# Graph attention on one core: a tile's mask, queries and residual input are loaded from ScalarE's DMA queue in place of SyncE's

## The reference

```python
def _L0_gnn_ref(node_matrix, adjacency_matrix, Wks, Wqs, Wvs, Wo):
    adj = jnp.maximum(adjacency_matrix, jnp.eye(n))
    keys, queries, values = (jnp.einsum('nj,hjk->hnk', node_matrix, W) for W in (Wks, Wqs, Wvs))
    atts = jnp.einsum('hqk,hmk->hqm', queries, keys) / key_dim ** 0.5
    atts = atts - 1e+16 * (1.0 - adj)[None, :, :]
    atts = jax.nn.softmax(atts, axis=-1)
    return jnp.einsum('hqm,hmk,hko->qo', atts, values, Wo)

x = _layernorm(x + _L0_gnn_ref(x, adj, ...), axis=-1)     # layer 0
...                                                        # layers 1 to 3 follow on x
```

## Time and profile before

| | |
|---|---|
| median of 3 runs | 2812.24 us (2811.44 to 2812.98) |
| the profiled execution | 2815.72 us, its span 2813.9 us |
| PE, DVE, ACT, POOL busy over the span | 90%, 55%, 49%, 41% |
| attention stage | some 208 to 1495 us of the span |
| DMA queue of the kernel, share of 16 engines | 69.6% of the span |

### The profile page before, as it was taken

One profiled execution on the slowest core, in us unless ns is written; L12 is line 12 of the kernel. 1 busy time (PEld: TensorE's weight loads), 2 busy tenths in 40 slices (PEclk: granted clock), 3 DMA queues, 4 the chain that ended last, 5 costly groups with the idle time before them and its releaser, 6 DMA issues. The chain is left out here.

```text
span 2813.9 us, 67215 instructions
## 1 busy us (share of the span) xinstructions
PE 2536.2 (90%) x24716; PEld 1564.6 (56%) x24716; DVE 1534.5 (55%) x2860; ACT 1388.6 (49%) x1848; POOL 1163.6 (41%) x879
## 2 busy tenths in 40 slices
PE   7998898988889888898996999799999999979998
PEld 6875566656666566565663444376444444434443
DVE  3447677766777677676772222354454555633222
ACT  3337677767777677676772322223333334323221
POOL 0007687767777677776780032200111111110232
PEclk9999899988999999998998999899999999989999
DMA  3118999999999999999994356411656667742554
GB/s 124 63 57 171 179 174 174 166 174 171 160 173 166 180 173 166 166 181 169 174 157 130 117 196 206 167 48 42 161 153 168 174 178 205 187 127 80 199 196 151
DMA packets 870507, 436.18 MB, mean 155 GB/s; under 512 B 791680, under 2 KB 810112, under 8 KB 859008
## 3 DMA queue, kind: packets, MB, share of 16 engines
q1 hardware_dynamic: 870272, 432.93, 69.6%
HBM read 201.15 MB, written 38.44 MB: 85 GB/s over the span
## 5 line engine op out<-in xcount | busy, mean ns | idle before, releaser
L603 POOL TENSOR_TENSOR att_part_low<-att_scores,att_part_high 128x1024 f16<-128x1024 f32 x352 | 665.7, 1894 | 291.1 <-ACT att_part_high L735 265.2
L766 DVE CUSTOM_DVE_ANT_0 att_scores<-att_slots,att_adj 128x1024 f32<-128x1024 f32 x528 | 568.3, 1092 | 185.8 <-PE att_slots L641 167.1
L719 ACT ACTIVATE att_scores<-att_scores,att_nmax 128x1024 f32<-128x1024 f32 x528 | 531.2, 1037 | 65.8 <-DVE att_nmax L776 63.2
L641 PE MATMUL att_slots<-l_kk,att_q 128*128 128x512 f16 x2112 | 499.8, 376 | 46.4 <-issue 29.0
L1300 PE MATMUL a_ps<-l_y,a_adj 128*128 128x512 f16 (+1 forms) x1936 | 431.6, 382 | 9.0 <-DVE a_adj L1314 4.7
L661 PE MATMUL att_ps_pv<-l_vv,att_far_high 128*128 128x65 f16 x4928 | 270.8, 197 | 115.2 <-DMA att_far_low<-att_part_low 114.8
L661 PEld LDWEIGHTS att_ps_pv<-l_vv,att_far_high 128*128 128x128 f16 x4928 | 258.2, 101 | 159.3 <-DMA att_far_low<-att_part_low 128.6
L1300 PEld LDWEIGHTS a_ps<-l_y,a_adj 128*128 128x128 f16 (+1 forms) x1936 | 183.1, 98 | 257.5 <-issue 42.4
L641 PEld LDWEIGHTS att_slots<-l_kk,att_q 128*128 128x128 f16 x2112 | 190.9, 102 | 223.2 <-issue 77.2
L809 DVE TENSOR_TENSOR att_near_low<-att_ps_t,att_near_high 128x512 f16<-128x512 f32 x352 | 225.7, 681 | 133.5 <-ACT att_near_high L746 133.2
L1045 PE MATMUL edge_ps_o<-l_sup,edge_pt_high 128*128 128x512 f16 x968 | 288.1, 379 | 0.0
(11 more groups left out here) (149 smaller groups left out, 3842.6 us busy)
## 6 DMA issues: line engine op xcount, KB each, us to landing
l_adj<-in_adj_cols SPq DMA_DIRECT2D x44, 1408.0 KB, 6.2
att_adj<-in_adj SPq DMA_DIRECT2D x22, 1354.0 KB, 6.8
l_adj_tiles<-in_adj SPq DMA_DIRECT2D x22, 1354.0 KB, 6.0
p_x_in<-x SPq DMA_DIRECT2D x66, 256.0 KB, 2.6
att_q<-q_rows SPq DMA_DIRECT2D x88, 128.0 KB, 6.1
a_xres<-x SPq DMA_DIRECT2D x44, 256.0 KB, 2.7
scores_rows<-edge_raw SPq DMA_DIRECT2D x8, 842.0 KB, 3.5
p_x_in<-in_x SPq DMA_DIRECT2D x22, 256.0 KB, 2.7
```

Of the source, the lines that this page charges most:

```text
L603: nc.gpsimd.tensor_tensor(out=part[1][:, v, lo:lo + width], in0=sc[:, v, lo:lo + width], in1=part[0][:, v, lo:lo + width], op=ALU.subtract ...
L641: mm = nc.tensor.matmul(slots[:, slot, z:z + w], q[:, u, h % 2, a, h // 2, :], kk[:, h, lo + z:lo + z + w], start=a == 0, stop=a == 1)
L719: nc.scalar.activation(sc[:, v, lo:lo + width], sc[:, v, lo:lo + width], ACT.Exp, bias=nmax[:, v:v + 1]).then_inc(exp_done, 1)
L766: nc.vector.tensor_tensor_reduce(out=sc[:, v, lo:lo + width], in0=slots[:, (NC * h + c) % 2, 0:width], in1=adj[:, u, lo:lo + width], scale ...
```

## The change

The mask, the queries and the residual input are issued by ScalarE, at the end of its step h = 1, behind that step's copies of the near part. SP keeps the loads of the first tile, the transposes, and the store at the start of step h = 1. The waits that guard the loads go along with them.

```diff
+        def load_q(queue, t, u):
+            for e in range(2):
+                for half in range(2):
+                    queue.dma_start(q[half * KD:half * KD + KD, u, e, :, :, :].rearrange("p a j r -> p (a j r)"),
+                                    q_rows[bass.ds(t * P + e * KD, KD), :]).then_inc(q_loaded[u], 16)
+
         @block.sync
         def _(sp):
...
-            def loads(m, u):
-                t = 2 * m + u
-                if not is_tile(m, u, T) and not is_tile(m, u, T - 1):
-                    m1, u1 = after(m, u)
-                    if not is_tile(m, u, 0):
-                        sp.wait_ge(slot_free, PER_TILE * t)
-                    sp.dma_start(adj[:, u1, 0:N], adj_rows[bass.ds((t + 1) * P, P), :]) \
-                        .then_inc(adj_loaded[u1], 16)
-                    load_q(t + 1, u1)
-                if not is_tile(m, u, 0):
-                    if not is_tile(m, u, 1):
-                        sp.wait_ge(misc_free, 2 * (t - 1))
-                    sp.dma_start(xres[:, :], x_rows[bass.ds((t - 1) * P, P), :]).then_inc(xres_loaded, 16)
-                    if not is_tile(m, u, 1):
-                        norm.store(sp, out_rows, *before(*before(m, u)))
-
             def step(m, u, h, on):
-                if h == 1:
-                    loads(m, u)
+                if h == 1 and not is_tile(m, u, 0) and not is_tile(m, u, 1):
+                    norm.store(sp, out_rows, *before(*before(m, u)))
...
         @block.scalar
         def _(act):
+            def loads(m, u):
+
+                t = 2 * m + u
+                if not is_tile(m, u, T) and not is_tile(m, u, T - 1):
+                    _m1, u1 = after(m, u)
+                    if not is_tile(m, u, 0):
+                        act.wait_ge(slot_free, PER_TILE * t)
+                    act.dma_start(adj[:, u1, 0:N], adj_rows[bass.ds((t + 1) * P, P), :]) \
+                        .then_inc(adj_loaded[u1], 16)
+                    load_q(act, t + 1, u1)
+                if not is_tile(m, u, 0):
+                    if not is_tile(m, u, 1):
+                        act.wait_ge(misc_free, 2 * (t - 1))
+                    act.dma_start(xres[:, :], x_rows[bass.ds((t - 1) * P, P), :]).then_inc(xres_loaded, 16)
...
+                if h == 1:
+                    loads(m, u)
                 if h == 5 and not is_tile(m, u, 0):
```

More of the change, by code:

```diff
@@ L579, in step @@
                                 .then_inc(far_ready[c][v], 16)
-            load_q(0, 0)
+            load_q(sp, 0, 0)
             sp.dma_start(adj[:, 0, 0:N], adj_rows[0:P, :]).then_inc(adj_loaded[0], 16)
```

## The result

The changed kernel takes 2869.73 us (median of 4 runs, 2855.52 to 2873.50) against 2811.84 us (4 runs, 2806.55 to 2812.98). The ratio is 1.020, with a 95% interval of 1.0163 to 1.0237. It is 58 us slower; the forecast was 31 us faster.

The account below looks back on a forecast made before the run. SP's queue was taken as the bound: 4.1 + 3.1 - 5.5 = 1.7 us a tile, 34 us over 20 tiles. 2815.7 - 34 + 3 = 2784.7, or 2781 us in the runs' terms; 8-in-10 range 2725 to 2868.

Parts of the forecast that it names:

- What bounds the kernel: In the attention stage SP's queue is the pacemaker, behind rather than waiting; TensorE is the second bound.
- Issue time leaves SP: Mask, queries and residual leave SP's queue, the store stays: 4.1 us a tile saved on SP.
- The stall of the next transposes: On SP after the loads: now 3.1 us a tile, replaced by at most 5.5 us, the upper bound taken.
- Six DMAs on ScalarE, covered: ScalarE's later work is delayed 3.9 us a tile, hidden while SP is late; 3 us added once for the first tile.
- The waits and the arrival: The moved mask and residual waits cost nothing on ScalarE; loads arrive in time even at twice their 10 us.
- The clock: TensorE's half-clock stretches after idling: a shorter stall may spare some, but nothing was counted.
- Rival A: ScalarE's DMAs wait for SP's transposes at descriptor making, holding ScalarE 11.3 us: 2858 to 2904, say 2865; chance 0.35.
- The 82 us: Sum if only the 4.1 us of issue on SP were saved, stall unchanged: 20 x 4.1.
- Rivals B and C: B: transposes pass freely, 2702, chance 0.12 for below 2745. C: no change, within 5.6 us of 2812, chance 0.13.

Follow-up runs that it names:

- the small loads: Changed kernel and kernel before, each moving a sixteenth of the loads' bytes from the third tile on: 2688.98 us on ScalarE's queue, 2762.97 on SP's.
- the quarters: Changed kernel with the mask in four back-to-back transfers at step 1: 2862.33 us, ratio 1.0180 against the kernel before.
- eighths: Changed kernel with loads spread over steps 1 to 5, the mask in eighths, four each at steps 1 and 2: 2777.26 us.
- halves: Loads spread over steps 1 to 5, half the mask each at 1 and 2: changed kernel (ScalarE's queue) 2803.87 us, kernel before (SP's) 2822.71.
- the last two kernels: Changed kernel, loads spread, mask in eighths: three, three, two at steps 1 to 3, 2745.80 us; two a step at steps 0 to 3, 2717.84.

## Why the prediction was wrong, point by point

*What bounds the kernel*: right. SP's queue sets the pace; taking 3 to 4 us of issue a tile off it without adding traffic gave 74 us (the small loads). All rows of transposes, loads and store on SP in the attention stage add up to 1092.5 us before and 1158.7 after, 66 us more for a kernel that is 58 us slower. In all 14 changed kernels without added waits or pauses this sum and the time moved by the same amount within 21 us, from 102 us less (2689) to 72 us more (the quarters, 2862).

*Issue time leaves SP*: right in size. From the end of the transpose ahead of the group to the start of the one behind it, 20 tiles take 102.7 us before and 28.6 after, 3.7 us less a tile where 4.1 was taken. At the median 1.0 us is left; twice the store was held and it was 4.7 and 5.3.

*The stall of the next transposes*: this step failed. It was sized at 5.5 us a tile and called an upper bound: the time of the loads' bytes at the best rate shown. That bound assumed that the bytes move at the rate that they reach alone. All 704 transpose rows add up to 1014.8 us on SP before and 1137.4 after. With small loads on SP they are 957.2, and 951.2 where loads and transposes are kept apart. So the loads' part was (1014.8 - 957.2) / 20 = 2.9 us a tile, as taken, and became (1137.4 - 957.2) / 20 = 9.0 us, not 5.5. Of the 9.0, 8.0 are the bytes, as small loads on ScalarE's queue leave 978.1. From the first far transpose to the last the stage grew by 54.7 us: the transposes hold SP 122.6 us longer, the stretches around loads and store (21 of them before, 20 after) are 75.4 shorter, and the other gaps 7.5 longer. With 9.0 in the place of 5.5 the prediction's own sum is 4.1 + 3.1 - 9.0 = -1.8 us a tile, 36 us slower; with the measured 3.7 and 2.9 for the other two it is -2.4, 48 us slower, of the 53.1 that the span grew.

*Six DMAs on ScalarE, covered*: right in the main. Predicted 3.9 us; they take 3.9 to 6.1 in a tile, 4.1 at the median, and 1.5 us of ScalarE's idle time. A pause of 3.7 us a tile alone cost 10 us in all, where 3 was counted.

*The waits and the arrival*: the loads came late, but nobody waited for the mask, the queries or the residual, other than once for the first tile's queries at the start (8.6 us, 9.0 before).

*The clock*: counted at nothing. The mean granted clock over the seventeen tiles is 0.91 against 0.92; TensorE's 7.13 us stand again ends at 1.2 GHz. This is a result of the stall, not a term of its own that was measured.

*Rival A*, given 0.35, had the sign and nearly the size (2865), but by luck, as the mechanism was another. Its DMAs on ScalarE would each have taken 1.5 us or more. The source view of the changed kernel:

```profile
L706 ACTq DMA_DIRECT2D att_adj<-in_adj x21: 334/346/393, 228.1 to 1430.9; - x21
L544 ACTq DMA_DIRECT2D att_q<-q_rows x84: 476/614/2351, 228.5 to 1433.9; - x84
L712 ACTq DMA_DIRECT2D att_xres<-in_x x22: 368/381/662, 281.5 to 1532.3; - x22
```

The median mask issue is 0.346 us, as on SP. The Trainium skill, "Perfetto Trace Analysis", "DMA Instruction — HWDGE (DVE, Sync)", has the descriptor generator locked for one instruction at a time; in these rows no waiting of that kind is to be seen beyond a few long query rows (up to 2.35 us, 2.17 on SP before). The other rule, "DMA: Bandwidth & Descriptors", "Issuing engines are not separate DMA queues", says that DMAs of several issuers interleave on the same 16 engines, and that a second issuer saves only issue time. The 82 us that the prediction worked out beside it did not come: for transposes on one queue and 2 MB of loads on the other the runs show a price that the rule does not name.

*Rivals B and C* did not come about. A gain of B's size is there once the bytes are gone (2689) or come in bursts short enough (2718).

*What stays open*: why the traffic slows when the two kinds meet. The trace shows mask packets of up to 9.29 us, not what they wait for. The packets of the transposes do not last longer themselves (16742 us in all on the 16 engines after, 16834 before), so the transposes are late by what stands between their packets. Whether packet size or spacing made eighths better than halves is open too, and whether the last two kernels gain by the burst alone: their DMAs also fall at other steps. Why queries and residual cost SP's queue more than the mask does was not looked into.

## What to carry to other kernels

Before loads are moved to a second queue, look at what the first queue still has in flight: a transfer's time alone is no upper bound for its cost beside another kind. Beside DMA transposes, a 2 MB burst of plain loads from another queue took 10.7 us for its mask in place of 6.3 apart from them, and held a transpose's issue for up to 11.4 us; one behind the other in one queue it was 6.8 us and at most 4.5. If the queue that is relieved carries transposes, cut the loads and spread them over the steps: with this the move's loss of 58 us became a gain of 88 us, though it is not shown how much the spreading would have given on the first queue.

## What the runs showed of the hardware that was not expected

- With transposes in one queue and large loads in the other, single packets of the loads hang: 140 of 2688 mask packets over 2 us, up to 9.29 us, where it was 3 of 2560 in one queue and none with the two kept apart.
- Windows of 2 us under 110 GB/s are common in both kernels (78 and 96 of 493), and mostly stand where a 16 KB instruction packet is in flight or just done. That it is the cause is not shown.
- Row size did not matter in a burst: 10.8 KB rows gave 2869.73 us, 2.7 KB rows 2862.33.
- ScalarE issues DMAs ahead of compute that stands before them in its program. The mask's issue starts at 813.47, and the near copies that come before it in the order start at 815.24. So six DMAs of 4.8 us cost ScalarE 2.03 us of its own time.
